# A convolution block in three stages: another order of the calls within a step of the attention stage, on TensorE, VectorE, ScalarE and GpSimd

## What is computed

```
queries = conv1x1_bn(x, wq, ...)  # 8 heads of 32
kv      = conv1x1_bn(x, wkv, ...) # 32 channels, keys and values
key, query = softmax(kv over pixels), softmax(queries over channels)
context  = einsum('bkn,bdn->bkd', key, kv)
attended = einsum('bkd,bhkn->bhdn', context, query)
x = x + conv1x1_bn(relu(attended), wp, ...)
hdn = relu(depthwise3x3(conv1x1_bn(x, w1, ...)) + bdw)
x = x + conv1x1_bn(hdn, w2, ...)
```

## Time and profile before

| what | value |
|---|---|
| median of 3 runs | 6704.27 us (6704.2 to 6706.16) |
| the profiled execution | 6705.41 us |
| its span | 6703.6 us, mean granted PE clock 0.981 |
| attention stage | from the start to about 1828 us |
| PE busy in 600 to 800 us | 190.70 of 200 us, granted clock 1.00 |
| DVE, ACT, POOL busy there | 142.28, 93.89, 77.74 us |

### The profile page before, as it was taken

How to read it: one execution, slowest core, us unless ns; L and a number is a source line. 1 busy time by engine, 2 the same in 40 slices (tenths; PEclk the granted TensorE clock), 3 DMA queues, 4 the chain that set the end, 5 groups by cost and what they waited for, 6 DMA issues and landing times. The chain is left out here.

```text
span 6703.6 us, 228614 instructions
## 1 busy us (share of the span) xinstructions
PE 6053.1 (90%) x96819; PEld 3479.4 (52%) x96819; DVE 5507.3 (82%) x8016; ACT 3811.1 (57%) x5690; POOL 4761.0 (71%) x3268
## 2 busy tenths in 40 slices
PE   7999999999779999999999999999999999996877
PEld 3444444444345555555555555655555665553333
DVE  5776776776578888888888888888888888886998
ACT  3444444444346666656666655666665666664776
POOL 2344333334258888888888888888888888886766
PEclk9999999999889999999999999999999999998999
DMA  1111111111100000010000010000001000001221
GB/s 30 43 46 41 53 43 46 46 42 47 34 26 3 3 3 3 3 44 3 3 3 3 3 35 13 3 3 3 3 3 44 3 3 3 3 3 50 71 75 52
DMA packets 115654, 157.60 MB, mean 24 GB/s; under 512 B 30512, under 2 KB 79952, under 8 KB 114768
## 3 DMA queue, kind: packets, MB, share of 16 engines
q1 hardware_dynamic: 114768, 144.38, 7.6%
HBM read 53.67 MB, written 52.79 MB: 16 GB/s over the span
## 5 line engine op out<-in xcount | busy, mean ns | idle before, releaser
L241 ACT ACTIVATE nn_yy<-nn_P 128x612 f32<-128x612 f32 x1200 | 817.0, 681 | 1656.8 <-DVE nn_P L330 1639.3
L397 PE MATMUL nn_P<-nn_hh,nn_w 64*64 64x256 f16 x38400 | 1534.8, 273 | 220.6 <-DVE nn_nl L341 107.1
L209 POOL TENSOR_TENSOR nn_hf<-nn_hf,nn_sr 128x512 f32<-128x512 f32 (+1 forms) x800 | 1439.9, 1821 | 155.4 <-DVE nn_sr L363 155.4
L220 POOL TENSOR_TENSOR nn_hl<-nn_hf,nn_hh 128x512 f16<-128x512 f32 (+1 forms) x768 | 1266.2, 1649 | 314.5 <-ACT nn_hh L253 306.3
L397 PEld LDWEIGHTS nn_P<-nn_hh,nn_w 64*64 64x64 f16 x38400 | 1022.7, 106 | 834.0 <-issue 664.7
L404 PE MATMUL nn_P<-nn_nh,nn_w 64*64 64x512 f16 x19200 | 1320.6, 379 | 77.6 <-DVE nn_nl L341 8.8
L330 DVE SCALAR_TENSOR_TENSOR nn_P<-nn_P,nn_xs 128x612 f32<-128x612 f32 x1200 | 960.4, 800 | 234.2 <-PE nn_P L397 209.6
L336 DVE TENSOR_TENSOR nn_P<-nn_P,nn_nh 128x612 f32<-128x612 f32 x1200 | 960.2, 800 | 213.2 <-ACT nn_nh L246 206.8
L397 PE MATMUL nn_P<-nn_hl,nn_w 64*64 64x256 f16 x19200 | 994.0, 270 | 1.5 <-issue 1.2
L341 DVE SCALAR_TENSOR_TENSOR nn_nl<-nn_P,nn_nh 128x612 f16<-128x612 f32 x1200 | 952.1, 793 | 34.3
L246 ACT ACTIVATE nn_nh<-nn_yy 128x612 f16<-128x612 f32 x1200 | 856.1, 713 | 37.9
(11 more groups left out here) (215 smaller groups left out, 7986.1 us busy)
## 6 DMA issues: line engine op xcount, KB each, us to landing
xn_scratch<-at_xb SPq DMA_DIRECT2D x128, 114.8 KB
nn_xs<-xn_scratch SPq DMA_DIRECT2D x48, 306.0 KB, 3.0
at_x<-in_x SPq DMA_DIRECT2D x32, 384.0 KB, 3.8
x_scratch<-at_x SPq DMA_DIRECT2D x64, 192.0 KB, 2.1
h_scratch<-nn_hf SPq DMA_DIRECT2D x48, 256.0 KB, 3.1
ml_xt<-x_scratch SPq DMA_DIRECT2D x32, 384.0 KB, 4.4
ml_ht<-h_scratch SPq DMA_DIRECT2D x128, 96.0 KB
out<-ml_ot SPq DMA_DIRECT2D x64, 192.0 KB, 2.1
```

The costliest lines, as they stand in the source:

```text
L209: e.tensor_tensor(hf[c][:, g, :], hf[c][:, g, :], sr[c][:, :].unsqueeze(1).broadcast_to((128, g.stop - g.start, A_COLS)), ALU.mult).then_i ...
L220: e.tensor_tensor(hl[c][:, g, :], hf[c][:, g, :], hh[c][:, g, :], ALU.subtract).then_inc(h_lo[n], 1)
L241: e.activation(half(yy[k % RING][:, :]), Pv[k % 2], ACT.Ln).then_inc(logged, 1)
L397: return pe.matmul(out[:, 0:AC, rows_y] if near else out[:, 1:BC, rows_y], w1[rows, wp, a, 1 if near else 0, k, cols], (hh, hl)[dp][u][row ...
```

## The change

In each of the four `step` functions the same calls stand in another order, and some take another image: a call that took `i1` in one step may now take `i2` in the next, which puts it later in the pipeline. No call is added, dropped or altered, and the SP queue keeps its list. The whole difference, context lines left out:

```diff
--- before.py
+++ after.py
@@ -784,10 +784,10 @@
-                i0, i1, i2, i3 = (image(n, p, t, 0), image(n, p, t, 1), image(n, p, t, 2), image(n, p, t, 3),)
-                hidden_low(i3, 3); x1_low(i2, 0); hidden_low(i3, 4); x1_low(i2, 1); hidden_low(i3, 5); e_low(i1, 0)
-                e_low(i1, 1); hidden_low(i2, 0); hidden_low(i2, 1); e_low(i1, 2); hidden_low(i2, 2); e_low(i1, 3); a_low(i1, 0)
-                a_low(i1, 1); a_low(i1, 2); x_low(i0); a_low(i1, 3)
+                i0, i1, i2, i3, = image(n, p, t, 0), image(n, p, t, 1), image(n, p, t, 2), image(n, p, t, 3)
+                hidden_low(i3, 2); a_low(i2, 2); a_low(i2, 3); x1_low(i2, 0); x1_low(i2, 1); hidden_low(i3, 3); hidden_low(i3, 4)
+                e_low(i1, 0); hidden_low(i3, 5); e_low(i1, 1); hidden_low(i2, 0); e_low(i1, 2); a_low(i1, 0); e_low(i1, 3); a_low(i1, 1)
+                x_low(i0); hidden_low(i2, 1)
@@ -886,13 +886,13 @@
-                i0, i1, i2 = (image(n, p, t, 0), image(n, p, t, 1), image(n, p, t, 2),)
-                x_high(i0); a_high(i1, 3); square(i2, 0); relu(i2, 4); x1_high(i1, 0); x1_high(i1, 1); log_var(i2, 0)
-                inv_root(i2, 0); relu(i2, 5); spread(i0, 0); k_exp(i0); spread(i0, 1); q_exp(i0, 0); relu(i1, 0); e_high(i0, 0)
-                q_exp(i0, 1); log_x(i2, 0); square(i2, 1); e_high(i0, 1); inv_x(i2, 0); relu(i1, 1); log_e(i0, 0); inv_e(i0, 0)
-                q_exp(i0, 2); e_high(i0, 2); log_e(i0, 1); inv_e(i0, 1); q_exp(i0, 3); e_high(i0, 3); log_var(i2, 1)
-                inv_root(i2, 1); relu(i1, 2); log_e(i0, 2); inv_e(i0, 2); a_high(i0, 0); a_high(i0, 1); log_x(i2, 1)
-                relu(i1, 3); inv_x(i2, 1); log_e(i0, 3); inv_e(i0, 3); a_high(i0, 2)
+                i0, i1, i2, i3, = image(n, p, t, 0), image(n, p, t, 1), image(n, p, t, 2), image(n, p, t, 3)
+                log_x(i3, 0); x_high(i0); q_exp(i1, 3); e_high(i1, 3); a_high(i1, 0); a_high(i1, 1); relu(i2, 1); inv_x(i3, 0)
+                log_e(i1, 2); inv_e(i1, 2); relu(i2, 2); square(i3, 1); log_var(i3, 1); inv_root(i3, 1); log_e(i1, 3); a_high(i1, 2)
+                inv_e(i1, 3); x1_high(i1, 0); a_high(i1, 3); x1_high(i1, 1); relu(i2, 3); relu(i2, 4); k_exp(i0); spread(i0, 0)
+                log_x(i3, 1); square(i2, 0); spread(i0, 1); log_var(i2, 0); inv_x(i3, 1); relu(i2, 5); inv_root(i2, 0); q_exp(i0, 0)
+                e_high(i0, 0); q_exp(i0, 1); e_high(i0, 1); log_e(i0, 0); q_exp(i0, 2); inv_e(i0, 0); relu(i1, 0); log_e(i0, 1)
+                e_high(i0, 2); inv_e(i0, 1)
@@ -1101,15 +1101,14 @@
-                i0, i1, i2, i3 = (image(n, p, t, 0), image(n, p, t, 1), image(n, p, t, 2), image(n, p, t, 3),)
-                refine_e(i1, 2); scale(i3, 1); affine(i3, 1); floor(i3, 1); x2_make(i2, 0); attended(i1, 2); hidden_high(i2, 3)
-                divide(i3, 0); sum_clamp(i3, 1); back_e(i1, 3); refine_e(i1, 3); attended(i1, 3); back_x(i3, 1); x1_make(i1, 0)
-                x1_make(i1, 1); hidden_high(i2, 4); var_a(i2, 0); var_b(i2, 0); k_max(i0); refine_root(i2, 0); q_max(i0, 0)
-                hidden_high(i2, 5); k_negate(i0); k_copy(i0); refine_x(i3, 1); scale(i2, 0); affine(i2, 0); q_max(i0, 1)
-                floor(i2, 0); k_place(i0); divide(i3, 1); k_inv(i0); context_scale(i0); block_diag(i0); x2_make(i2, 1)
-                sum_clamp(i2, 0); back_x(i2, 0); refine_x(i2, 0); back_e(i0, 0); hidden_high(i1, 0); refine_e(i0, 0)
-                hidden_high(i1, 1); attended(i0, 0); back_e(i0, 1); refine_e(i0, 1); hidden_high(i1, 2); attended(i0, 1)
-                var_a(i2, 1); var_b(i2, 1); refine_root(i2, 1); back_e(i0, 2)
+                i0, i1, i2, i3, = image(n, p, t, 0), image(n, p, t, 1), image(n, p, t, 2), image(n, p, t, 3)
+                affine(i3, 1); x1_make(i1, 1); k_max(i0); floor(i3, 1); k_negate(i0); hidden_high(i2, 3); q_max(i0, 0); k_copy(i0)
+                divide(i3, 0); hidden_high(i2, 4); sum_clamp(i3, 1); q_max(i0, 1); k_place(i0); k_inv(i0); back_x(i3, 1); var_a(i2, 0)
+                refine_x(i3, 1); var_b(i2, 0); context_scale(i0); refine_root(i2, 0); block_diag(i0); divide(i3, 1); hidden_high(i2, 5)
+                scale(i2, 0); back_e(i0, 0); refine_e(i0, 0); affine(i2, 0); attended(i0, 0); floor(i2, 0); hidden_high(i1, 0)
+                back_e(i0, 1); x2_make(i2, 1); refine_e(i0, 1); attended(i0, 1); sum_clamp(i2, 0); hidden_high(i1, 1); back_e(i0, 2)
+                x1_make(i0, 0); refine_e(i0, 2); hidden_high(i1, 2); attended(i0, 2); back_e(i0, 3); var_a(i2, 1); var_b(i2, 1)
+                back_x(i2, 0); refine_e(i0, 3); attended(i0, 3); refine_root(i2, 1); scale(i2, 1); refine_x(i2, 0); x2_make(i1, 0)
@@ -1241,14 +1240,13 @@
-                i0, i1, i2 = (image(n, p, t, 0), image(n, p, t, 1), image(n, p, t, 2),)
-                project(i1, 0); conv(i2, 4, 2); centring(i2, 0); conv(i2, 5, 0); project(i1, 1); variance(i2, 0); conv(i2, 5, 1)
-                keys(i0); conv(i2, 5, 2); q_rows(i0, 0); conv(i1, 0, 0); q_rows(i0, 1); conv(i1, 0, 1); mlp_out(i2, 1)
-                k_turn(i0); conv(i1, 0, 2); x_sum(i2, 0); q_cols(i0, 0); conv(i1, 1, 0); context(i0); q_cols(i0, 1)
-                conv(i1, 1, 1); q_cols(i0, 2); centring(i2, 1); conv(i1, 1, 2); e_sum(i0, 0); conv(i1, 2, 0); q_cols(i0, 3)
-                variance(i2, 1); conv(i1, 2, 1); e_sum(i0, 1); conv(i1, 2, 2); mix(i0, 0); conv(i1, 3, 0); mix(i0, 1)
-                conv(i1, 3, 1); e_sum(i0, 2); conv(i1, 3, 2); mix(i0, 2); conv(i1, 4, 0); mlp_out(i1, 0); e_sum(i0, 3)
-                conv(i1, 4, 1); x_sum(i2, 1); mix(i0, 3)
+                i0, i1, i2, i3, = image(n, p, t, 0), image(n, p, t, 1), image(n, p, t, 2), image(n, p, t, 3)
+                variance(i3, 0); conv(i2, 0, 1); q_cols(i1, 0); q_cols(i1, 1); context(i1); q_cols(i1, 2); conv(i2, 0, 2); conv(i2, 1, 0)
+                q_cols(i1, 3); e_sum(i1, 0); conv(i2, 1, 1); conv(i2, 1, 2); e_sum(i1, 1); mix(i1, 0); mlp_out(i3, 1); mix(i1, 1)
+                x_sum(i3, 0); conv(i2, 2, 0); conv(i2, 2, 1); e_sum(i1, 2); conv(i2, 2, 2); centring(i3, 1); project(i1, 0); e_sum(i1, 3)
+                variance(i3, 1); mix(i1, 2); conv(i2, 3, 0); mix(i1, 3); conv(i2, 3, 1); conv(i2, 3, 2); conv(i2, 4, 0); mlp_out(i2, 0)
+                conv(i2, 4, 1); project(i1, 1); keys(i0); conv(i2, 4, 2); q_rows(i0, 0); conv(i2, 5, 0); conv(i2, 5, 1); x_sum(i3, 1)
+                q_rows(i0, 1); conv(i2, 5, 2); centring(i2, 0); conv(i1, 0, 0); k_turn(i0)
```

## The result

| | before | after |
|---|---|---|
| median of the runs | 6705.22 us (4 runs, 6704.2 to 6709.22) | 6645.95 us (4 runs, 6643.04 to 6654.61) |
| the profiled execution, its span | 6705.41, 6703.6 us | 6643.04, 6641.2 us |
| attention stage, to the first instruction of `nnmf` | 1828.1 us | 1760.7 us |
| `nnmf`, to the first load of `token_mlp` | 4328.8 us | 4325.9 us |
| `token_mlp`, to the end of the span | 546.7 us | 554.6 us |

The ratio is 0.9913 (95% interval 0.9895 to 0.9930), 0.9% faster. The time forecast was 6640, in a range of 6628 to 6672.

What follows compares the result with a forecast made beforehand. PE was taken to bound the kernel, its waits removable: steps of 51.6 us, 2.45 less, give -71 over 29 steps, and the ends +7. 6705.4 - 71 + 7 = 6641.4, against the median 6640 us; range 6628 to 6672.

Steps and rivals of the forecast that it cites:

- Step 1: First conv matmul waiting for SP's shifted copies: 11.4 us of other PE work, slack 3.1, all 22.7 us gained.
- Steps 2 and 3: Second `project` waiting for `a_low`, `centring` for `sum_clamp`: slack over 2 and about 1, gaining 9.3 and 10.6 us.
- Step 4: New tight place, `variance` through ACT and DVE to first `e_sum`: at most 9.6 us against 9.55, slack 0.2.
- Step 5: Second `e_sum` behind POOL's `hidden_low` and `e_low`: 13.3 against 13.2 us, no slack, 0.1 or 0.2 us wait.
- Step 6: From `attended` to the last `mix`: 0.5 us left over.
- Filling: Image 0 passing alone: two chains run one after the other, `keys` of image 1 at about 82; +3.3 us.
- Draining: Stage end: a stall goes (4.6 us), but the last image's `centring` and `variance` follow its last conv; +3.7 us.
- (a): Rival: the first two `e_sum` wait 0.5 to 1.5 us each step; 6669 us at 1.0 more; chance 0.21.
- (b): Rival: from `variance` to `e_sum`, DVE's two-input calls each lose a full POOL turn; 6721 us, slower; chance 0.06.
- (c): Rival: PE's waits move to places thought to have slack, 2.4 us in all; 6704 us; chance 0.03.
- A: Experiments' theory, distances: waits went because more other PE work stands between a call and the one awaiting its result.
- B: Experiments' theory, free turns: waits went because DVE no longer waits for POOL inside its calls.

Runs made afterwards that it cites:

- Experiment 2: Changed kernel with one PE call moved: the next image's first conv part goes back ahead of the last two parts; 6724.7 us.
- experiment 3: Changed kernel with DVE's `divide` and `scale` moved ahead of `block_diag`, on which the first `e_sum` waits; 6665.19 us.
- experiment 5: Changed kernel with ACT's last `relu` and DVE's last `hidden_high` of an image moved forward, in every step; 6659.72 us.
- experiment 6: Changed kernel with two POOL calls changed round: the second quarter's `e_low` ahead of the last conv tile's `hidden_low`; 6648.15 us.
- experiment 4: Changed kernel with POOL's `x_low` done twice, first into a spare tile nobody reads; 6676.16 us.
- Experiment 8: Changed kernel, steady lists untouched, with other lists of calls only for the first image alone and the last images' steps; 6642.58 us, ratio 0.9904.
- experiment 1: Kernel before with one DVE move: `back_x` of the second half behind both `x1_make`; 6697.97 us, ratio 0.9991.

## Why the prediction came out as it did

The account was right: PE bounds the stage, the waits were the only time to be had, and they went. Step 51.34 against 51.6 forecast, no wait of PE against 0.1 or 0.2 a step, time 6646 against 6640. Point by point:

- **Bound.** PE's own work was put at 54.05 - 2.64 = 51.4; it is 51.34. The waits had been divided by 19, the number of stalls, but 1000 us hold 18.5 steps of 54.05: (42.6 + 47 x 0.16) / 18.5 = 2.71, and 54.05 - 2.71 = 51.34.
- **Step 1** (copies to convolution): 11.61 us of other work against 11.4, slack 3.2 against 3.1. Experiment 2 shows that without this distance the gain is gone, however free DVE's turns are; how much of the 2.71 this step brought by itself, no run separates.
- **Steps 2 and 3** (`a_low` to `project`, `sum_clamp` to `centring`): both waits are gone, as expected. No run moved these two alone, so that their own distances did it is argued and not shown.
- **Step 4** (`variance` to `e_sum`): mis-sized. The chain took 1017.80 to 1026.35 = 8.55 us, not 9.3 to 9.6: the one lost turn was there, at `refine_root` and at 0.81, which is what 9.3 had for it (9.3 - 8.5). But the prediction added up whole durations, and calls in a row overlap: `var_a`, `refine_x` and `var_b` last 0.68 or 0.69 and start 0.60 apart, `block_diag` takes 1.63 from start to end instead of 1.79, and `variance` to `var_a` 3.54 instead of 3.71. And `e_sum` came 9.82 after `variance`, not 9.55. Slack 1.27 instead of 0.2; experiments 3, 5 and 6 put it between 0.96 and 1.5.
- **Step 5** (second `e_sum`): POOL's second `e_low` was done at 1030.34 and `e_sum` started at 1031.19: slack 0.85 instead of none. That is step 4's error carried on.
- **Step 6** (`attended` to the last `mix`): 0.5 forecast, and right. In the changed kernel the third `attended` is done at 994.52, 0.58 us before the last `mix`:

```profile
993.83 0.69 DVE L1095 SCALAR_TENSOR_TENSOR at_a<-at_PA,at_sr 128x512 f32<-128x512 f32 x1 [0.32 <-issue]
```

```profile
995.10 0.81 PE L1230 MATMUL at_PA<-at_e,at_bd 128*128 128x512 f16 x3
```

  The 1.1 of experiment 4 is more because DVE also had idle time ahead of that `attended` (0.32 here), which its lost turns used up first.
- **Steady sum.** 29 x 2.71 = 78.6 instead of 71; the difference is the 0.2 of new waits that didn't come and 0.06 of PE's own work.
- **Filling**: the term that was mis-sized. +3.3 was forecast, +8.5 measured. PE's timeline while the first image runs alone answers to the earlier trace rows:

```profile
65.54 0.59 PE L1223 MATMUL at_PA<-at_e,at_ones_k 128*128 128x512 f16 x2 [2.51 <-DVE at_st L1082]
...
73.92 2.79 PE L1239 MATMUL at_PB<-at_a,at_wpT 128*96 128x512 f16 x6 [3.97 <-POOL at_a L776]
...
84.43 2.79 PE L1239 MATMUL at_PB<-at_a,at_wpT 128*96 128x512 f16 x6 [4.57 <-POOL at_a L776]
87.16 1.70 PE L1172 MATMUL at_PA<-at_x,at_wkvT 97*32 97x512 f16 x6
```

  The prediction had the right cause, that the two chains from `mix` to `project` now run one after the other, and too low a price: in the kernel before one `project` waited 1.57 here, now both wait, 3.97 and 4.57, and the second `e_sum` waits 2.51 for DVE where it was 1.29. Other waits became shorter: between the `keys` of image 0 and those of image 1 PE is idle for 17.4 us instead of 9.9. That is 7.5 of the 8.5; the other 1.0 is busy time (24.7 instead of 23.7), at a somewhat lower granted clock (0.84 instead of 0.86). Experiment 8 takes 5.1 of the 8.5 back by order alone. The wait ahead of the convolution, which was to stay at 4.41, is 1.39 (with 2.10 ahead of a `q_rows` that was not there before).
- **Draining**: the last conv part to the end of the last `divide`, forecast 32 instead of 23. PE and then DVE, answering to the earlier trace rows:

```profile
1718.42 0.38 PE L1136 MATMUL at_PC<-at_xr,at_w1T 105*128 105x512 f16 x1
...
1729.29 3.90 PE L1147 MATMUL at_PL<-at_hd,at_w2T 128*96 128x512 f16 x9 [7.86 <-POOL at_hd L764]
...
1744.67 2.02 PE L1164 MATMUL at_PL<-at_xm,at_sum_w 96*96 96x512 f32 x2 [6.46 <-DVE at_xm L1004]
```

```profile
1748.91 1.29 DVE L1040 TENSOR_TENSOR at_xb<-at_nd,at_nr 96x192 f32<-96x192 f32 x4
```

  `mlp_out` starts 10.9 us after it (11 forecast) and the whole takes 31.8 us. Step and place were right, and so was the size: 2.8 us without the work that was moved there, where 3.7 was forecast.
- **Together**: the ends cost 78.6 - 67.4 = 11.2 (8.5 and some 2.8) instead of 7, inside its bounds of 0 to 14. So the attention stage gained 67.4 against 64 forecast; `nnmf` (-2.9) and `token_mlp` (+7.9) bring the profiled execution to 6643.04, 1.6 above the 6641.4 of the sum. That it came so near is partly luck: the steady steps gave 7.6 us more than forecast, the ends took 4.2 more, and the two other stages, put at nothing, took 5.0. That the median lies another 3 above it is within the scatter of single executions, 6643 to 6655.

**The rivals.** (a), tight places that stall, is what experiments 3 and 5 look like when 1.8 and 1.9 us are added to the chain of step 4; the change itself stays 1.27 clear of it. (b), slower through lost turns in that chain: `refine_root` lost one turn, `refine_x`, `var_b` and the subtractions none. Experiment 5 shows the mechanism to be real and its price small: four casts lost 1.87 us and the step grew by 0.53, since most of it was covered. (c), nothing gained, had no part.

**Which theory.** A: one distance cut to 6.3 us costs 2.52 although DVE's turns stay as free as they were (experiment 2), while 2.0 us of lost turns taken away in the kernel before give 0.27 (experiment 1), and 0.96 put into the changed one cost nothing (experiment 6). B is the second condition: where the distance left is short, at `block_diag` and at the last `mix`, lost turns beyond some 1.3 to 1.5 or 1.1 us reach PE (experiments 5 and 4). For the waits of steps 2 and 3 this stays argued.

## What to carry to other kernels

When one engine bounds a pipelined loop, look for the wait at its end: how much of the bounding engine's own other work stands between the call that starts a chain and the call that waits for it. Contention inside another engine's calls costs nothing until it has used up the slack of that chain, and a change in the order elsewhere can bring it back: a late producer may be what keeps a rival engine idle at the right moment. Steady lists and the lists of the first and last iterations want different orders; give the ends lists of their own.
